# State-space layer: products and scans of four states at a time, through a buffer in SBUF

## The chip, the cores and the metric

The kernel runs on one core of a Trainium2 chip. The metric is the device time of one execution in microseconds (us), the median of several runs. TensorE is PE in the profile, VectorE is DVE, ScalarE is ACT, GpSimd is POOL.

## What is computed

The whole program is an image model of four layers. Only the attention half of layer 2 is touched, a bidirectional state-space (Mamba) layer on 8 images of 257 tokens with 512 inner channels and 32 states:

```python
dt = jax.nn.softplus(jnp.einsum('blr,dr->bld', x_dbl[..., :DT_RANK], Wdt) + bdt)
A = -jnp.exp(Alog)
def step(h, ins):
    dt_t, B_t, C_t, u_t = ins
    dA = jnp.exp(dt_t[..., None] * A)
    h = dA * h + (dt_t * u_t)[..., None] * B_t[:, None, :]
    y = jnp.einsum('bdn,bn->bd', h, C_t)
    return (h, y)
```

It runs once forward and once on the reversed tokens, so there are 16 units of one image and one direction.

## The kernel before, in words

`section_mamba` handles the 16 units one after the other. Channels lie on the 128 partitions in four groups (`j`), states in four groups of eight (`q`). A chunk `n` = 4q + j is eight states of one channel group, 16 chunks to a unit (`NCH`). A chunk is cut into four pairs of states (`m`), and p = 4n + m counts the 64 of them (`SUB`). Each state is a row of L = 256 tokens, so two states are 512 elements on each partition and one PSUM bank.

For two states p, in the steady loop:

- ACT (`decay`, L2326) writes dA = exp(dt * A) into `da`, double-buffered by chunk. The first element of each row stays zero, so that one scan can run over several states in a row.
- PE (`spread_b`, L2114) spreads B over the partitions into the PSUM bank `pb[:, p % 4]` with two matmuls, one for each state. It works two p ahead of the sums that it does for chunk n - 2. It waits on `b_free` for the bank.
- DVE (`product`, L2494) multiplies that bank in place by dt * u (`dtu2`, in SBUF). It does p + 1 ahead of scan p.
- DVE (`body`, L2513) runs the recurrence as a scan of 512 elements: first input `da` in SBUF, second input `pb` in PSUM, output `hs` in SBUF. Before the first scan of chunk n it waits on `hc_done` for POOL to be through with chunk n - 2. The scan raises `b_free`, on which PE, ACT and POOL wait.
- POOL (L2013) multiplies four states of `hs` (1024 elements) by C (`cb`, in SBUF) into `hc`. Both inputs lie in SBUF. There are two to a chunk, and a copy of the last token (L2012) beside them. Between them POOL does other work for the next unit (`taps` L1935, `cut` L1941, `cut_low` and `soften` L1949 to L1960) and for the last token (L1974 to L1995), all of it with SBUF inputs.
- PE (`total`, L2127) adds the states of `hc` into `py` by identity matmuls, two chunks later; its end raises `y_free`, on which POOL waits for the `hc` buffer.

Turned pairs of states are the exception: for m = 3 in state groups q = 1, 2 and 3 (12 of 64 p), DVE makes no product. ACT (`products`, L2348) forms B * dt * u in the other orientation, and PE (`turn_products`, L2101) turns it into `pb` with four transposes of 128x128; the scan reads it from PSUM like the others. `made(p)` counts the products that DVE has made, for the waits on `b_set`.

The order on each engine is written out by hand. Every queue is in order. SP alone issues the DMAs of the layer (`load_c`, `store_c`).

Of the kernel before, what the change touches and what calls it, by code (L numbers as in the profile page):

```python
# [104 lines left out]
def section_constants(nc, k, cls_tok):  # L105
    with nc.Block() as block:
        @block.sync
        def _(sp):
            sp.dma_start(k.cls[:], cls_tok).then_inc(k.loads, 16)
            sp.wait_ge(k.loads, 16)  # L110

        @block.vector
        def _(dve):
            nc.vector.memset(k.ones[:], 1.0)
            nc.vector.memset(k.mean[:], 1.0 / D)
            nc.vector.memset(k.eps[:, 0:1], 1e-5)
# [1665 lines left out]
def section_mamba(nc, k, con, dirs, bfuse, normed=0):  # L1782
# [8 lines left out]
    with ExitStack() as ctx:  # L1791
# [32 lines left out]
        names = ("w_first w_in w_ready eye_set rates in_back out_back proj_done proj_free lead uc_done xd_done xd_out part_set part_cut stacked last_bc last_out rate_l decay_l sum_l y_last z_last dt_done "  # L1824
                 "dt_free dt_exp dt_set crow_in c_out c_even c_odd dtut_done dtut_in tp_in b_done b_free da_done b_set hc_done y_free ys_done o_done o_out "
                 "sqd var std scaled normed f_done f_out conv_link soft_link soft_low soft_top last_link act_head act_tail").split()
# [13 lines left out]
        def made(p):  # L1840
            return sum(not turned(i) for i in range(p + 1))

# [32 lines left out]
        with nc.Block() as block:  # L1875
# [43 lines left out]
            def _(pool):  # L1919
# [77 lines left out]
                def body(u, v, d, before, after):  # L1997
                    scanned, summed = Turn(u, SUB, 4), Turn(u, NCH, 2)
                    for n in range(NCH):
# [49 lines left out]
            def _(pe):  # L2049
# [43 lines left out]
                def turn_products(u, v, p):  # L2093

                    q, j = p // 4 // DJ, p // 4 % DJ
                    if j == 0:
                        pe.wait_ge(s["tp_in"], Turn(u, len(TURNED))(TURNED.index(q) + 1))
                    pe.wait_ge(s["b_free"], Turn(u, SUB, 4)(p - 3))
                    for o in range(2):
                        for h in range(2):  # L2100
                            ins = nc.tensor.transpose(pb[:, p % 4, o, h * P:h * P + P], tp[:, TURNED.index(q) % 2, o, h, j * P:j * P + P], k.ident[:])  # L2101
                    ins.then_inc(s["b_done"], 1)

                def spread_b(u, v, p):

                    if turned(p):
# [4 lines left out]
                    pe.wait_ge(s["b_free"], Turn(u, SUB, 4)(p - 3))  # L2111
# [3 lines left out]
                    ins.then_inc(s["b_done"], 1)  # L2115

# [122 lines left out]
            def _(act):  # L2239
# [78 lines left out]
                def decay(u, v, d, n, m, free):  # L2318
# [3 lines left out]
                    if free is not None:  # L2322
                        act.wait_ge(s["b_free"], free)
                    for o in range(2):
# [13 lines left out]

                def products(u, v, q, o, free):

                    if o == 0:
# [7 lines left out]
                    if o:  # L2349
                        ins.then_inc(s["tp_in"], 1)  # L2350

# [4 lines left out]
                def body(u, v, d, before, after):  # L2356
                    for n in range(NCH):
# [12 lines left out]
                        for m in range(4):  # L2370
                            free = Turn(u, SUB, 4)(4 * (n - 1) + m + 1) if n or before is not None else None
# [6 lines left out]
                        if n == 1:  # L2378
                            for o in range(2):
                                products(u, v, 1, o, Turn(u, SUB)(0) if before is not None else None)  # L2380
                        if n in (5, 7):
                            products(u, v, 2, n // 2 - 2, Turn(u, SUB)(0) if before is not None else None)
                        if n in (9, 10):
                            products(u, v, 3, n - 9, Turn(u, SUB)(32))
                        if after is not None:
# [53 lines left out]
            def _(dve):  # L2439
# [17 lines left out]

                dve.sem_inc(s["b_free"], 4)
                dve.sem_inc(s["y_free"], 2)
# [26 lines left out]

                def product(u, v, p):

                    j = p // 4 % DJ
                    if p < 4 * DJ and p % 4 == 0:  # L2490
                        dve.wait_ge(s["dt_set"], Turn(u, DJ)(j + 1))
                    b2 = pb[:, p % 4]
                    dve.wait_ge(s["b_done"], Turn(u, SUB)(p + 1))
                    nc.vector.tensor_tensor(b2, b2, dtu2[:, v, j:j + 1, 0:L].broadcast_to([P, 2, L]), ALU.mult).then_inc(s["b_set"], 1)  # L2494

                def body(u, v, d, before, after):
                    for n in range(NCH):
                        for m in range(4):
                            p = 4 * n + m
                            if p + 1 < SUB:  # L2500
                                if not turned(p + 1):
                                    product(u, v, p + 1)
                            elif after is not None:
                                product(u + 1, 1 - v, 0)
                            if m == 0:
                                dve.wait_ge(s["hc_done"], Turn(u, 2 * NCH, 16)(2 * n - 2))
                            dve.wait_ge(s["da_done"], Turn(u, SUB)(p + 1))
                            if turned(p):
                                dve.wait_ge(s["b_done"], Turn(u, SUB)(p + 1))
                            else:  # L2510
                                dve.wait_ge(s["b_set"], Turn(u, made(SUB - 1))(made(p)))
                            two = lambda ap: ap.rearrange("p s t -> p (s t)")
                            nc.vector.tensor_tensor_scan(two(hs[:, n % 2, 2 * m:2 * m + 2, :]), two(da[:, n % 2, 2 * m:2 * m + 2, :]), two(pb[:, p % 4]), 0.0, ALU.mult, ALU.add).then_inc(s["b_free"], 1)  # L2513
                            if before is not None:
# [857 lines left out]
def build(nc, a, out, last):  # L3372
    with ExitStack() as ctx:
# [5 lines left out]
        k.x = sb("x", [P, C, B, T])  # L3379
        k.xb = sb("xb", [P, C, TP])  # L3380
        k.cls = sb("cls", [P, C])
# [3 lines left out]
        k.eps = sb("eps", [P, 2])  # L3385
        k.junk = sb("junk", [P, P])
        k.ln_cen, k.ln_sq, k.ln_rstd = sb("ln_cen", [P, C, T]), sb("ln_sq", [P, C, T]), sb("ln_rstd", [P, T])
# [171 lines left out]
```

## Time and profile before

| | us |
|---|---|
| median of 3 runs | 3766.42 (3755.68 to 3770.4) |
| the profiled execution, its own time | 3768.24 |
| its span, first to last instruction | 3766.3 |
| the state-space stage in it, first to last scan and sum | about 1804 (1164.5 to 2968.8) |

The page gives each engine's busy time and share of the span, then the span in 40 slices, in tenths. A group of instructions is written as line, engine, operation, output <- inputs, shape, count, busy time, mean ns of one, idle time of the engine before them and what ended it. [...] Shares over the whole span mix stages with different limits, so the stage has its own windows.

### The profile page before, as it was taken

The page shows a single profiled execution, that of the slowest core. Times are in us where ns is not written, and L with a number is a line of the kernel's source. Part 1 is how long each engine was busy: PE and PEld are TensorE (multiplying, and loading weights), DVE is VectorE, ACT ScalarE, POOL GpSimd, SP SyncE. Part 2 cuts the span into 40 slices and gives each one's busy share as a digit, 9 for nine tenths or more (in the row PEclk, how much of TensorE's full clock was granted, in tenths as well). Part 3 has the DMA queues.
Part 4 walks back from the last instruction along what each step waited for, and adds up shares of the span by engine and source line. Part 5 has one row for each costly group of instructions (what it writes and reads, how often), then busy time and mean ns, then how long its engine had stood idle before and what let it go on. Part 6 is the DMA issues. An engine that isn't in the chain of part 4 may idle for free. (4 is left out here: it accounts for less than half of the span.)

```text
span 3766.3 us, 60909 instructions
## 1 busy us (share of the span) xinstructions
PE 3211.5 (85%) x19844; PEld 2404.9 (64%) x19844; DVE 2513.4 (67%) x3795; ACT 2065.8 (55%) x4488; POOL 1935.6 (51%) x1702
## 2 busy tenths in 40 slices
PE   0959989989986888988888888888988789999767
PEld 0649976668974666666666666666765565666534
DVE  6341136643126999999999999999999644666531
ACT  0332225551227777877777777877776434666511
POOL 0023312101317888889888889898888400000054
PEclk9879989999987999999999999999999998999955
DMA  3039820014951111111111111111111000000045
GB/s 103 2 143 334 323 92 2 2 42 147 333 180 34 46 35 36 46 35 36 46 48 35 49 35 35 47 35 35 46 35 34 23 15 1 2 2 2 18 129 153
DMA packets 133788, 262.81 MB, mean 70 GB/s; under 512 B 14000, under 2 KB 104360, under 8 KB 122952
## 3 DMA queue, kind: packets, MB, share of 16 engines
q1 hardware_dynamic: 122120, 227.64, 18.3%
q0 software_dynamic: 11328, 30.95, 2.5%
q8 instruction: 175, 2.87, 0.3%
q14 instruction: 165, 1.35, 0.1%
HBM read 232.03 MB, written 26.51 MB: 69 GB/s over the span
## 5 line engine op out<-in xcount | busy, mean ns | idle before, releaser
L2013 POOL TENSOR_TENSOR ssm_hc<-ssm_hs,ssm_cb 128x1024 f32<-128x1024 f32 x512 | 1205.2, 2358 | 177.8 <-PE ssm_py L2127 157.8
L2513 DVE TENSOR_TENSOR_SCAN ssm_hs<-ssm_da,ssm_pb 128x512 f32<-128x512 f32 x1024 | 1220.2, 1206 | 97.1 <-POOL ssm_hc L2013 92.4
L2127 PE MATMUL ssm_py<-ssm_hc,ident 128*128 128x256 f32 x4096 | 1071.1, 384 | 40.3 <-POOL ssm_hc L2013 40.3
L2326 ACT ACTIVATE ssm_da<-ssm_dt,ssm_an 128x255 f32<-128x255 f32 x2048 | 863.2, 498 | 191.5 <-DVE ssm_hs L2513 152.4
L2127 PEld LDWEIGHTS ssm_py<-ssm_hc,ident 128*128 128x128 f32 x4096 | 711.4, 192 | 121.1 <-POOL ssm_hc L2013 48.3
L2494 DVE TENSOR_TENSOR ssm_pb<-ssm_pb,ssm_dtu 128x512 f32<-128x512 f32 x832 | 562.7, 676 | 48.3 <-PE ssm_pb L2114 23.8
L2114 PE MATMUL ssm_pb<-ssm_bst,ssm_eyeb 96*128 96x256 bf16 x1664 | 329.1, 280 | 137.3 <-DVE ssm_hs L2513 115.7
L2114 PEld LDWEIGHTS ssm_pb<-ssm_bst,ssm_eyeb 96*128 96x128 bf16 x1664 | 133.8, 99 | 342.7 <-DVE ssm_hs L2513 239.3
L3339 DVE TENSOR_TENSOR moe_hid<-moe_pu,moe_actg 128x512 f32<-128x512 f32 x71 | 49.1, 691 | 349.0 <-PE moe_pu L2982 349.0
L2982 PEld LDWEIGHTS moe_pu<-moe_xt,moe_up 128*128 128x128 f32 x2272 | 267.0, 193 | 6.4 <-ACT moe_xt L3102 3.0
L2982 PE MATMUL moe_pu<-moe_xt,moe_up 128*128 128x128 f32 x2272 | 268.0, 277 | 1.8 <-ACT moe_xt L3102 1.8
L2853 POOL DMA_INDIRECT moe_xr<-moe_x_dram,moe_rowx x71 | 69.0, 971 | 334.6 <-PE ln_ps L2970 179.9
L1662 DVE TENSOR_REDUCE duo_mxr<-duo_pairs 128x4 f32<-128x1024 f32 x128 | 156.6, 1224 | 101.6 <-PE duo_pairs L1400 78.8
L1570 ACT ACTIVATE duo_ex<-duo_pairs 128x1024 f32<-128x1024 f32 x128 | 131.0, 1024 | 99.3 <-PE duo_pairs L1400 99.2
L1396 PE MATMUL duo_pairs<-duo_k,duo_q 32*128 32x256 f32 x1024 | 152.0, 414 | 9.1 <-DVE duo_mxr L1662 3.7
L2101 PE MATMUL ssm_pb<-ident,ssm_tp 128*128 128x128 f32 x768 | 118.8, 278 | 47.8 <-ACT ssm_tp L2348 34.4
L1400 PE MATMUL duo_pairs<-duo_q,duo_k 32*128 32x256 f32 x1024 | 146.3, 402 | 1.2 <-ACT duo_ex L1570 1.1
L2101 PEld LDWEIGHTS ssm_pb<-ident,ssm_tp 128*128 128x128 f32 x768 | 91.7, 141 | 79.4 <-DVE ssm_hs L2513 51.1
L2058 PE MATMUL ln_ps<-x,ssm_win 128*128 (+1 forms) x512 | 135.1, 388 | 3.5 <-DVE x L351 1.8
L2994 PE MATMUL ln_ps<-moe_down,moe_hid 128*128 128x256 f32 x568 | 134.5, 380 | 1.1 <-ACT moe_yo L3120 1.1
L2859 POOL DMA_INDIRECT moe_y_dram<-moe_yo,moe_rowy x71 | 70.2, 988 | 118.9 <-ACT moe_yo L3120 118.9
L2348 ACT ACTIVATE ssm_tp<-ssm_dtut,ssm_bt 128x512 f32<-128x512 f32 x192 | 125.2, 708 | 0.0
(591 smaller groups left out, 5279.1 us busy)
## 6 DMA issues: line engine op xcount, KB each, us to landing
moe_up<-in_moe_up SPq DMA_DIRECT2D x72, 1024.0 KB, 5.4
ssm_cb<-ssm_c_dram SPq DMA_DIRECT2D x64, 1024.0 KB, 5.6
moe_down<-in_moe_down SPq DMA_DIRECT2D x72, 512.0 KB, 6.2
sw_wt<-in_sw_w SPq DMA_DIRECT2D x47, 192.5 KB
moe_x_dram<-moe_tok SPq DMA_DIRECT2D x32, 128.0 KB
moe_yg<-moe_y_dram SPq DMA_DIRECT2D x16, 256.0 KB, 3.4
tok_w<-in_wd SPq DMA_DIRECT2D x4, 576.0 KB, 13.0
out<-h SPq DMA_DIRECT2D x1, 2056.0 KB, 6.3
```

What stands on the lines that cost most here:

```text
L1396: ins1 = nc.tensor.matmul(dst1[:, o, at], q[r, b1, t * P:t * P + P], kk[r, b1, a, 0:256], start=True, stop=True)
L1400: ins2 = nc.tensor.matmul(dst2[:, o, at], kk[r, b2, a, t * P:t * P + P], q[r, b2, 0:256], start=True, stop=True)
L1662: released(nc.vector.tensor_reduce(mxr[:, u % 2, a, 2 * jp:2 * jp + 2, :], bank("s1", u, a, jp).rearrange("p o (t s) -> p o t s", t=2), AX ...
L2013: nc.gpsimd.tensor_tensor(hc[:, n % 2, part_], hs[:, n % 2, part_], cb[:, q % 2, part_, :], ALU.mult).then_inc(s["hc_done"], 1)
L2058: ins = nc.tensor.matmul(pm[:, n % 2, 0:T], w_in[:, c, n * P:n * P + P], row, start=(c == 0), stop=(c == C - 1))
L2101: ins = nc.tensor.transpose(pb[:, p % 4, o, h * P:h * P + P], tp[:, TURNED.index(q) % 2, o, h, j * P:j * P + P], k.ident[:])
L2114: ins = nc.tensor.matmul(pb[:, p % 4, o, :], one_state(st), bst2[:, v, 0:L], start=True, stop=True)
L2127: ins = nc.tensor.matmul(sums(j), k.ident[:], hc[:, n % 2, st, :], start=False, stop=(q == QN - 1 and st == NQ_ - 1 and j % 2 == 1))
L2326: ins = nc.scalar.activation(da[:, n % 2, 2 * m + o, 1:L], dt2[:, v, j, 1:L], ACT.Exp, scale=a_n[:, d, j, st:st + 1])
L2494: nc.vector.tensor_tensor(b2, b2, dtu2[:, v, j:j + 1, 0:L].broadcast_to([P, 2, L]), ALU.mult).then_inc(s["b_set"], 1)
L2513: nc.vector.tensor_tensor_scan(two(hs[:, n % 2, 2 * m:2 * m + 2, :]), two(da[:, n % 2, 2 * m:2 * m + 2, :]), two(pb[:, p % 4]), 0.0, ALU.m ...
L2982: ins = nc.tensor.matmul(pu[:, b % 2, g, j * P:j * P + P], up[:, b % WR, c, g * HID + j * P:g * HID + j * P + P], xt[:, b % 2, c, :], star ...
```

## The change

Scans and products are made for four states (1024 elements, two PSUM banks) instead of two. r counts these half chunks, 32 to a unit (`PAIRS`). The product reads two banks of `pb` and writes a new SBUF buffer `bs` of two halves; the scan takes its second input from `bs`. Turned half chunks are those with r odd in state groups q = 1 and 3, 8 of 32: for them the scan reads the two banks of `pb` straight, and ACT and PE turn four states instead of two. DVE waits ahead of product r + 1 until scan r - 1 is complete, because it writes the buffer which that scan reads. PE waits for its banks on `b_set` (the product has read them) where a product is made, and on `scanned` where it is turned. `scanned` replaces `b_free` for ACT and POOL. The buffers `xb` and `junk`, which nothing reads, and the memset of `xb` at the start go.

```diff
-            nc.vector.memset(k.xb[:], 0.0)
...
+        bs = sb("bs", [P, 2, 4, L])
...
-        TM = 3
-        TURNED = (1, 2, 3)
+        PAIRS = SUB // 2
+        TURNED = (1, 3)
...
-        def turned(p):
-            return p % 4 == TM and p // 4 // DJ in TURNED
+        def turned(r):
+            return r % 2 == 1 and r // 2 // DJ in TURNED
...
-                            pool.wait_ge(s["b_free"], scanned(4 * n + 2 * half + 2))
+                            pool.wait_ge(s["scanned"], scanned(2 * n + half + 1))
...
+                def bank_free(u, r):
+                    if r < 2:
+                        if not (isinstance(u, int) and u == 0):
+                            pe.wait_ge(*((s["scanned"], Turn(u, PAIRS)(0)) if r else (s["b_set"], Turn(u, made(PAIRS - 1))(0))))
+                    elif turned(r - 2):
+                        pe.wait_ge(s["scanned"], Turn(u, PAIRS)(r - 1))
+                    else:
+                        pe.wait_ge(s["b_set"], Turn(u, made(PAIRS - 1))(made(r - 2)))
...
-                    st = q * NQ_ + 2 * TM + o
-                    for h in range(2):
-                        ins = nc.scalar.activation(tp[:, TURNED.index(q) % 2, o, h, :], dtut[:, h, :], ACT.Copy, scale=bt[:, v, h, st:st + 1])
+                    for o in range(2):
+                        st = q * NQ_ + 4 + 2 * i + o
+                        for h in range(2):
+                            ins = nc.scalar.activation(tp[:, i, o, h, :], dtut[:, h, :], ACT.Copy, scale=bt[:, v, h, st:st + 1])
...
-                    nc.vector.tensor_tensor(b2, b2, dtu2[:, v, j:j + 1, 0:L].broadcast_to([P, 2, L]), ALU.mult).then_inc(s["b_set"], 1)
+                    dve.wait_ge(s["b_done"], Turn(u, PAIRS)(r + 1))
+                    if r >= 2 or not (isinstance(u, int) and u == 0):
+                        dve.wait_ge(s["scanned"], Turn(u, PAIRS)(r - 1))
+                    spread = pb[:, at:at + 2].rearrange("p g s t -> p (g s) t")
+                    nc.vector.tensor_tensor(bs[:, r % 2], spread, dtu2[:, v, j:j + 1, 0:L].broadcast_to([P, 4, L]), ALU.mult).then_inc(s["b_set"], 1)
...
+                def scan(u, r):
+                    n, half = r // 2, r % 2
+                    if half == 0:
+                        dve.wait_ge(s["hc_done"], Turn(u, 2 * NCH, 16)(2 * n - 2))
+                    dve.wait_ge(s["da_done"], Turn(u, SUB)(2 * r + 2))
+                    if turned(r):
+                        dve.wait_ge(s["b_done"], Turn(u, PAIRS)(r + 1))
+                        steps = pb[:, 2:4].rearrange("p g s t -> p (g s t)")
+                    else:
+                        dve.wait_ge(s["b_set"], Turn(u, made(PAIRS - 1))(made(r)))
+                        steps = bs[:, half].rearrange("p s t -> p (s t)")
+                    four = lambda ap: ap[:, n % 2, 4 * half:4 * half + 4, :].rearrange("p s t -> p (s t)")
+                    nc.vector.tensor_tensor_scan(four(hs), four(da), steps, 0.0, ALU.mult, ALU.add).then_inc(s["scanned"], 1)
...
+                    for r in range(PAIRS):
+                        n = r // 2
+                        if r + 1 < PAIRS:
+                            if not turned(r + 1):
+                                product(u, v, r + 1)
+                        elif after is not None:
+                            product(u + 1, 1 - v, 0)
+                        scan(u, r)
```

## Rows read from the trace of the kernel before

**Rows 1.** The page: busy time of the engines, then DVE and POOL in 40 slices.

```profile
PE 3211.5 (85%) x19844; PEld 2404.9 (64%) x19844; DVE 2513.4 (67%) x3795; ACT 2065.8 (55%) x4488; POOL 1935.6 (51%) x1702
...
DVE  6341136643126999999999999999999644666531
...
POOL 0023312101317888889888889898888400000054
```

**Rows 2.** Busy time by engine: the stage, one unit, and a stretch far from it.

```profile
1164.50:2968.80 1804.30, 1563.27 (x7956) 1177.53 (x7957) 1686.26 (x1975) 1343.59 (x3036) 1588.80 (x1177) 0.98 0.13 38
1277.30:1390.30 113.00, 97.50 (x505) 73.67 (x504) 105.64 (x125) 85.46 (x193) 100.53 (x76) 1.00 0.13 38
3580.00:3670.00 90.00, 59.32 (x198) 34.80 (x196) 27.77 (x56) 14.86 (x42) 46.70 (x48) 0.52 0.43 125
```

**Rows 3.** Groups of instructions over the span, costliest first.

```profile
L2013 POOL TENSOR_TENSOR ssm_hc<-ssm_hs,ssm_cb 128x1024 f32<-128x1024 f32 x512 | 1205.2, 2358 | 177.8 <-PE ssm_py L2127 157.8
L2513 DVE TENSOR_TENSOR_SCAN ssm_hs<-ssm_da,ssm_pb 128x512 f32<-128x512 f32 x1024 | 1220.2, 1206 | 97.1 <-POOL ssm_hc L2013 92.4
L2494 DVE TENSOR_TENSOR ssm_pb<-ssm_pb,ssm_dtu 128x512 f32<-128x512 f32 x832 | 562.7, 676 | 48.3 <-PE ssm_pb L2114 23.8
L2348 ACT ACTIVATE ssm_tp<-ssm_dtut,ssm_bt 128x512 f32<-128x512 f32 x192 | 125.2, 708 | 0.0
```

**Rows 4.** DVE in order of time, inside a unit: start, us, instruction.

```profile
1510.57 0.68 DVE L2494 TENSOR_TENSOR ssm_pb<-ssm_pb,ssm_dtu 128x512 f32<-128x512 f32 x1
1511.16 1.21 DVE L2513 TENSOR_TENSOR_SCAN ssm_hs<-ssm_da,ssm_pb 128x512 f32<-128x512 f32 x1
1512.28 0.68 DVE L2494 TENSOR_TENSOR ssm_pb<-ssm_pb,ssm_dtu 128x512 f32<-128x512 f32 x1
1512.87 1.21 DVE L2513 TENSOR_TENSOR_SCAN ssm_hs<-ssm_da,ssm_pb 128x512 f32<-128x512 f32 x1
```

**Rows 5.** One line each: duration ns min/median/max, first and last start, shape.

```profile
L276 DVE TENSOR_TENSOR tok_pix<-tok_lo,tok_hi x2: 1217/1221/1225, 65.3 to 67.6; 128x1024 f32<-128x1024 f32 x2
...
L3166 DVE SCALAR_TENSOR_TENSOR x<-x,moe_sc,moe_rstd x16: 472/946/1600, 185.8 to 221.6; 128x257 f32<-128x257 f32 x16
...
L2494 DVE TENSOR_TENSOR ssm_pb<-ssm_pb,ssm_dtu x832: 669/674/700, 1158.8 to 2964.7; 128x512 f32<-128x512 f32 x167
...
L2513 DVE TENSOR_TENSOR_SCAN ssm_hs<-ssm_da,ssm_pb x1024: 1190/1207/1222, 1164.5 to 2967.5; 128x512 f32<-128x512 f32 x171
...
L2013 POOL TENSOR_TENSOR ssm_hc<-ssm_hs,ssm_cb x512: 2337/2357/2379, 1170.0 to 2969.2; 128x1024 f32<-128x1024 f32 x171
```

**Rows 6.** An earlier stage in order of time, DVE beside POOL.

```profile
190.28 0.69 DVE L3163 TENSOR_TENSOR moe_xn<-x,moe_rstd 128x514 f32<-128x514 f32 x1 [2.09 <-ACT moe_rstd L3052]
...
191.01 1.42 DVE L3166 SCALAR_TENSOR_TENSOR x<-x,moe_sc,moe_rstd 128x257 f32<-128x257 f32 x1
...
191.06 1.09 POOL L2846 TENSOR_TENSOR h<-h,moe_xn 128x514 f32<-128x514 f32 x1 [3.74 <-DVE moe_xn L3163]
...
192.35 0.47 DVE L3166 SCALAR_TENSOR_TENSOR x<-x,moe_sc,moe_rstd 128x257 f32<-128x257 f32 x1
```

**Rows 7.** Just before the stage: POOL beside a DVE tensor_scalar, both ways.

```profile
1131.76 1.49 DVE L2455 TENSOR_SCALAR ssm_skip<-ident,ssm_cols 128x128 f32<-128x128 f32 x2
...
1133.05 1.33 POOL L1935 TENSOR_TENSOR ssm_e<-ssm_e,ssm_dt 128x514 f32<-128x514 f32 x1
...
1135.87 1.27 POOL L1935 TENSOR_TENSOR ssm_e<-ssm_e 128x514 f32<-128x514 f32 x1
```

**Rows 8.** Matmul groups of PE in one unit (1277.3 to 1390.3).

```profile
L2127 PE MATMUL ssm_py<-ssm_hc,ident 128*128 128x256 f32 x256 | 66.0, 379 | 2.9 <-POOL ssm_hc L2013 2.9
L2114 PE MATMUL ssm_pb<-ssm_bst,ssm_eyeb 96*128 96x256 bf16 x104 | 20.2, 276 | 8.6 <-DVE ssm_hs L2513 8.3
...
L2101 PE MATMUL ssm_pb<-ident,ssm_tp 128*128 128x128 f32 x48 | 7.4, 276 | 3.0 <-ACT ssm_tp L2348 2.3 <-DVE ssm_hs L2513 0.7
```

More of the change, by code:

```diff
@@ L1824, in section_mamba @@
         names = ("w_first w_in w_ready eye_set rates in_back out_back proj_done proj_free lead uc_done xd_done xd_out part_set part_cut stacked last_bc last_out rate_l decay_l sum_l y_last z_last dt_done "
-                 "dt_free dt_exp dt_set crow_in c_out c_even c_odd dtut_done dtut_in tp_in b_done b_free da_done b_set hc_done y_free ys_done o_done o_out "
+                 "dt_free dt_exp dt_set crow_in c_out c_even c_odd dtut_done dtut_in tp_in b_done scanned da_done b_set hc_done y_free ys_done o_done o_out "
                  "sqd var std scaled normed f_done f_out conv_link soft_link soft_low soft_top last_link act_head act_tail").split()
@@ L1830, in section_mamba, with made @@
         SUB = 4 * NCH
-        TM = 3
-        TURNED = (1, 2, 3)
+        PAIRS = SUB // 2
+        TURNED = (1, 3)
         def sums(j):
             return py[:, j // 2, j % 2 * L:j % 2 * L + L]
-        def turned(p):
-            return p % 4 == TM and p // 4 // DJ in TURNED
-        def made(p):
-            return sum(not turned(i) for i in range(p + 1))
+        def turned(r):
+            return r % 2 == 1 and r // 2 // DJ in TURNED
+        def made(r):
+            return sum(not turned(i) for i in range(r + 1))
         def image(u, d):
@@ L1997, in body @@
                 def body(u, v, d, before, after):
-                    scanned, summed = Turn(u, SUB, 4), Turn(u, NCH, 2)
+                    scanned, summed = Turn(u, PAIRS), Turn(u, NCH, 2)
                     for n in range(NCH):
@@ L2093, in turn_products @@
                 def turn_products(u, v, p):
-                    q, j = p // 4 // DJ, p // 4 % DJ
+                    q, j, i = p // 4 // DJ, p // 4 % DJ, p % 2
                     if j == 0:
-                        pe.wait_ge(s["tp_in"], Turn(u, len(TURNED))(TURNED.index(q) + 1))
-                    pe.wait_ge(s["b_free"], Turn(u, SUB, 4)(p - 3))
+                        pe.wait_ge(s["tp_in"], Turn(u, 2 * len(TURNED))(2 * TURNED.index(q) + i + 1))
                     for o in range(2):
                         for h in range(2):
-                            ins = nc.tensor.transpose(pb[:, p % 4, o, h * P:h * P + P], tp[:, TURNED.index(q) % 2, o, h, j * P:j * P + P], k.ident[:])
-                    ins.then_inc(s["b_done"], 1)
+                            ins = nc.tensor.transpose(pb[:, p % 4, o, h * P:h * P + P], tp[:, i, o, h, j * P:j * P + P], k.ident[:])
+                    if i:
+                        ins.then_inc(s["b_done"], 1)
+                def bank_free(u, r):
[6 more added lines that the diff above has]
+                        pe.wait_ge(s["b_set"], Turn(u, made(PAIRS - 1))(made(r - 2)))
                 def spread_b(u, v, p):
-                    if turned(p):
+                    r = p // 2
+                    if p % 2 == 0:
+                        bank_free(u, r)
+                    if turned(r):
                         turn_products(u, v, p)
@@ L2110, in spread_b @@
                         pe.wait_ge(s["stacked"], u + 1)
-                    pe.wait_ge(s["b_free"], Turn(u, SUB, 4)(p - 3))
                     for o in range(2):
@@ L2114, in spread_b @@
                         ins = nc.tensor.matmul(pb[:, p % 4, o, :], one_state(st), bst2[:, v, 0:L], start=True, stop=True)
-                    ins.then_inc(s["b_done"], 1)
+                    if p % 2:
+                        ins.then_inc(s["b_done"], 1)
                 def total(u, v, d, n, m):
@@ L2322, in decay @@
                     if free is not None:
-                        act.wait_ge(s["b_free"], free)
+                        act.wait_ge(s["scanned"], free)
                     for o in range(2):
@@ L2337, in take_steps, with products @@
                         nc.scalar.copy(dtut[:, h, :], pm[:, h, :]).then_inc(s["dtut_in"], 1)
-                def products(u, v, q, o, free):
-                    if o == 0:
+                def products(u, v, q, i, free):
+                    if i == 0:
                         act.wait_ge(s["last_out"], u + 1)
@@ L2345, in products @@
                             act.wait_ge(s["b_done"], free)
-                    st = q * NQ_ + 2 * TM + o
-                    for h in range(2):
-                        ins = nc.scalar.activation(tp[:, TURNED.index(q) % 2, o, h, :], dtut[:, h, :], ACT.Copy, scale=bt[:, v, h, st:st + 1])
-                    if o:
-                        ins.then_inc(s["tp_in"], 1)
+                    for o in range(2):
+                        st = q * NQ_ + 4 + 2 * i + o
+                        for h in range(2):
+                            ins = nc.scalar.activation(tp[:, i, o, h, :], dtut[:, h, :], ACT.Copy, scale=bt[:, v, h, st:st + 1])
+                    ins.then_inc(s["tp_in"], 1)
                 def decay_last(u):
@@ L2370, in body @@
                         for m in range(4):
-                            free = Turn(u, SUB, 4)(4 * (n - 1) + m + 1) if n or before is not None else None
+                            free = Turn(u, PAIRS)(2 * (n - 1) + m // 2 + 1) if n or before is not None else None
                             if n + 1 < NCH:
@@ L2377, in body @@
                             take_steps(u)
[L2378 to L2384, printed above, removed]
+                        if n in (1, 2):
+                            products(u, v, 1, n - 1, Turn(u, PAIRS)(0) if before is not None else None)
+                        if n in (8, 10):
+                            products(u, v, 3, n // 2 - 4, Turn(u, PAIRS)(PAIRS // 2))
                         if after is not None:
@@ L2456, in _ @@
                 ins.then_inc(s["w_ready"], 1)
-                dve.sem_inc(s["b_free"], 4)
                 dve.sem_inc(s["y_free"], 2)
@@ L2485, in add, with product @@
                     ins.then_inc(s["f_out"], 1)
-                def product(u, v, p):
-                    j = p // 4 % DJ
-                    if p < 4 * DJ and p % 4 == 0:
+                def product(u, v, r):
+                    j, at = r // 2 % DJ, 2 * (r % 2)
+                    if r < 2 * DJ and r % 2 == 0:
                         dve.wait_ge(s["dt_set"], Turn(u, DJ)(j + 1))
-                    b2 = pb[:, p % 4]
-                    dve.wait_ge(s["b_done"], Turn(u, SUB)(p + 1))
-                    nc.vector.tensor_tensor(b2, b2, dtu2[:, v, j:j + 1, 0:L].broadcast_to([P, 2, L]), ALU.mult).then_inc(s["b_set"], 1)
@@ L2496, in body @@
-                def body(u, v, d, before, after):
[L2497 to L2513, printed above, removed]
+                    dve.wait_ge(s["b_done"], Turn(u, PAIRS)(r + 1))
@@ new lines, in product @@
+                    if r >= 2 or not (isinstance(u, int) and u == 0):
[7 more added lines that the diff above has]
+                    dve.wait_ge(s["da_done"], Turn(u, SUB)(2 * r + 2))
+                    if turned(r):
+                        dve.wait_ge(s["b_done"], Turn(u, PAIRS)(r + 1))
[5 more added lines that the diff above has]
+                    nc.vector.tensor_tensor_scan(four(hs), four(da), steps, 0.0, ALU.mult, ALU.add).then_inc(s["scanned"], 1)
@@ L2514, in body @@
+                def body(u, v, d, before, after):
+                    for r in range(PAIRS):
[6 more added lines that the diff above has]
+                        scan(u, r)
+                        for m in (2 * (r % 2), 2 * (r % 2) + 1):
                             if before is not None:
@@ L3379, in build @@
         k.x = sb("x", [P, C, B, T])
-        k.xb = sb("xb", [P, C, TP])
         k.cls = sb("cls", [P, C])
@@ L3385, in build @@
         k.eps = sb("eps", [P, 2])
-        k.junk = sb("junk", [P, P])
         k.ln_cen, k.ln_sq, k.ln_rstd = sb("ln_cen", [P, C, T]), sb("ln_sq", [P, C, T]), sb("ln_rstd", [P, T])
```

## The prediction

> **What bounds the kernel now.** I read the page first: DVE is busy 67% of the span, but nine tenths and more in every slice of the state-space stage, where POOL shows eight tenths [rows 1]. The change touches that stage alone, so the whole-span shares decide nothing. The windows say it in numbers: in 1804.3 us of stage DVE is busy 1686, POOL 1589, PE 1563 and ACT 1344; in one unit of 113 us they are 105.6, 100.5, 97.5 and 85.5 [rows 2]. DVE is the bound; POOL, with 88%, is close behind, and what DVE still idles before its scans is 92 us in which it waits for POOL's product with C [rows 3]. The reader should keep two facts: DVE and POOL are the two fullest engines, and they work beside each other almost all the time. Anything that keeps them from working at the same time costs the sum of both instead of the larger one.
>
> **The change, part by part.** *Fewer, longer DVE instructions.* A product of 512 elements takes 676 ns, a tensor_tensor of 1024 elements takes 1221 [rows 3, 5], so 512 more elements cost about 0.54 us and 0.14 us is fixed. A scan of 512 takes 1206 ns [rows 3]; no longer one is in the trace. With the same fixed 0.14 its elements cost 1.065 us, and 1024 of them give 2.27; twice the row, 2.41, is the upper end, and I take 2.27. But neighbours overlap: from product start to next product start it is 1.71 us [rows 4], 0.59 and 1.12, so in the chain a fixed cost of only some 0.05 us is left of each. Per unit DVE has now 52 products and 64 scans, 52 x 0.59 + 64 x 1.12 = 102.4 us. Then it has 24 products and 32 scans, 24 x 1.12 + 32 x 2.19 = 97.0. That is 5.4 us less per unit.
>
> *DVE's new wait on itself.* Product r + 1 waits for scan r - 1, the instruction directly in front of it, and behind it on DVE stands scan r, which POOL waits for. The nearest row is a dependent pair: L3163 starts at 190.28 and takes 0.69, L3166 waits for it and starts at 191.01, 0.04 behind its end [rows 6], where undisturbed neighbours start 0.1 ahead of it [rows 4]. So it costs about 0.12 us x 24 = 2.9 us per unit; the bounds are 0 and 0.2 x 24 = 4.8. The Trainium skill, "VectorE: DVE Perf Modes", section "The DRAIN you can't avoid", says that a semaphore between DVE instructions costs nothing extra; by that the DVE chain would be 2.9 us per unit shorter than I count. The rows here speak for a small cost.
>
> *The scan's second input moves from PSUM to SBUF.* This carries the sum. Before, each DVE instruction in the loop has one input in SBUF and one in PSUM, and it runs beside POOL with no effect on either: 832 products lie between 669 and 700 ns, 1024 scans between 1190 and 1222, 512 POOL products between 2337 and 2379 [rows 5]. In an earlier stage a DVE instruction with both tensors in SBUF meets a POOL tensor_tensor, and there it is different. The same L3166 on 257 elements takes 0.47 us alone and 1.42 beside POOL; it starts at 191.01, POOL at 191.06 and ends at 192.15, and DVE ends at 192.43, 0.28 later, which is the time that 257 elements stream [rows 6]. So DVE stood still until POOL's instruction was through. The trace holds 16 instructions of L3166, 9 of them beside POOL, and 8 of those 9 took 1.4 to 1.6 us, of all 16 the shortest took 472 ns and the longest 1600 [rows 5]. It goes the other way too: two DVE tensor_scalar end at 1133.25, POOL's L1935 started at 1133.05 and took 1.33 instead of 1.27 us [rows 7]. 0.20 us of overlap cost it 0.06, so 0.14 us of its start is hidden and after that it waits. Both engines thus exclude each other for their streaming time.
>
> After the change 24 of a unit's 32 scans have `da` and `bs`, both in SBUF, and all of POOL's arithmetic reads SBUF. If the scan behaves like L3166, these 384 scans and POOL's work share one resource. A scan holds it for what streams, 2.27 - 0.14 + 0.02 = 2.15 us. POOL is busy 1588.8 us in the stage [rows 2], of which only 5 us are memsets. The sum is 1588.8 + 384 x 2.15 = 2414 us. What makes it less: while a scan holds, the 0.14 us start of the next POOL instruction hides, at most 384 x 0.14 = 54. What makes it more: where POOL has nothing queued it sees the scan's semaphore about 0.1 us late, at most 384 x 0.1 = 38, and the scan may count with its full 2.27, 46 more. So the stage takes 2361 to 2499. Mostly POOL will have something queued, since the 8 scans from PSUM in a unit go beside it and let DVE run ahead until the two `hs` buffers are full; I take 30 hidden and 20 of idle, 2405 us, 150 per unit. The stage grows by 2405 - 1804 = 601 us.
>
> The rule speaks for the step from L3166 to a scan, which no row shows: the Trainium skill, "SBUF — State Buffer", section "Who interferes with whom", says that a DVE instruction with two SBUF inputs contends with a GpSimd instruction that reads SBUF, since its second input comes through the read interface that both share, and whoever is second blocks fully. The trace agrees as far as it goes [rows 6]. By the rule the sum is as above; without it, the next part's 3731.
>
> *What hides under that.* DVE's own work per unit, 24 x 1.21 + 32 x 2.27 = 102 us plus 3 for the small ones, lies under 150. PE makes 96 instead of 104 spreads and 64 instead of 48 transposes; by their rows 20.2/104 and 7.4/48 us [rows 8] that is -1.6 + 2.5, so 0.9 us more on 97.5. ACT makes 16 instead of 12 turned copies of 0.71 us [rows 3], 2.8 more on 85.5. Both have over 45 us of room per unit. If the cover were gone (no exclusion), DVE at about 103 plus waits would still lie above both. The new waits of PE stand ahead of `spread_b`, with the sums of chunk n - 2 queued behind; a product is read out one scan earlier than before, so they come early except for turned half chunks. There PE has from the end of scan r - 2 one scan and one product, 3.4 us, for 8 transposes and 4 sums, 8 x 0.155 + 4 x 0.26 = 2.3 us, which fits. No DMA changes. The memset of `xb` lies at the very start, where DVE then waits for the image; I cost it at nothing (0 to 0.7 us).
>
> **Sum.** 3768.2 for the profiled execution, which is 1.8 above the median of the runs shown, + 601 = 4369. I predict 4370.
>
> **The rivals.** *No exclusion for a scan (12%).* For it: the scan takes two cycles or so per element, 1065 ns for 512, so it is another program than L3166, and no row shows a scan with two SBUF inputs. Against it: L3166 and tensor_scalar, two different operations, are both held. Then DVE saves 5.4 - 2.9 = 2.5 us per unit, 40 in all, with the idle before its scans as it is: 3768 - 40 = 3728 by the sum, 3731 with what a late turned half chunk may cost, 0.2 us per unit. The range of this case is 3680 (no wait on itself, 5.4 x 16 less) to 3790 (scans at 2.41 us: 32 x 0.14 x 16 = 72 more). This is the rival on the other side: it turns on one thing, whether the 24 scans per unit reach SBUF past POOL.
>
> *Partial exclusion (5%).* A scan that takes an element only every second cycle could leave POOL every other turn. Half of the 601 us would then stand: 4070. Against it: L3166 waited for the full POOL instruction, not for parts of it.
>
> *Exclusion, and TensorE's clock falls (5%).* PE would be busy 98 of 150 us. In a stretch where PE is busy 59 of 90 us the granted clock is 0.52, near the 1.2 GHz level; in the stage it is 0.98, near 2.4 GHz [rows 2]. With a mean of 0.6, PE would need 98 / 0.6 = 163 us per unit and be the bound: 3768 + 16 x (163 - 113) = 4568. Against it: a slower PE is busy more of the time, and its gaps here would be a few us at most. It decides from a granted clock of about 98 / 150 = 0.65 down.
>
> **How the numbers follow.** Exclusion with PE in time has 78%, with its own range of 4290 to 4480: the bounds of the sum are 3768 + 557 = 4325 and 3768 + 695 = 4463, and I add 20 to 35 for uneven turns. The range that should hold 8 in 10 is 4150 to 4570; it takes in the third rival, and leaves out the first, the second and some of the likeliest. Half a percent is about what a measurement of this kernel can tell from no change, here 19 us. Slower by more has 78 + 5 + 5 = 88% and 1 from the first rival's top, 89; faster by more (below 3748) has 8, no change 3, from the first rival.
>
> **What would show it.** If right: the 8 scans per unit from `pb` keep about 2.27 us, while those from `bs` show 3 to 4.6 us, often ending one scan's streaming time behind a POOL instruction; POOL's product with C shows a mean well above 2358 ns, 3 to 4.5 us; windows over the stage show DVE and POOL both over 90% busy though a unit takes about 150 us; PE and ACT fall to 65% and 59%. If the first rival holds, scans from `bs` and `pb` are equally long and POOL's stays at 2358. If the third holds, PE's granted clock in the stage is below 0.65 and DVE waits for `b_done`. The forecast is wrong in size if a scan of 1024 elements isn't near 2.27 us or if POOL idles much while DVE makes products.

## The result and the profile after

| | before | after |
|---|---|---|
| median | 3768.41 us (4 runs, 3755.68 to 3771.11) | 4464.9 us (4 runs, 4460.09 to 4486.24) |
| span of the profiled execution | 3766.3 us | 4458.9 us |
| state-space stage, first to last scan | 1804 us | 2498 us |

The ratio is 1.186 with a 95% interval of 1.182 to 1.189. The kernel became slower by 696 us; 601 were forecast. The stage grew by 694 us, which is the whole difference. A unit takes 157.0 us instead of 113.

Windows over the stage and over one unit of the changed kernel (length; busy us and count of PE, PEld, DVE, ACT, POOL; granted TensorE clock; DMA share; GB/s) answer to [rows 2]:

```profile
1159.40:3657.90 2498.50, 1779.12 (x8072) 1353.52 (x8073) 1979.30 (x1014) 1390.97 (x3098) 2150.75 (x1175) 0.87 0.09 28
1316.20:1473.10 156.90, 112.63 (x514) 85.65 (x514) 124.34 (x65) 88.54 (x197) 137.13 (x76) 0.88 0.09 28
```

POOL has the same instructions as before but is "busy" for 2151 us in the stage instead of 1589. It did not get more work: its instructions last longer. The same is seen in the groups (line numbers are shifted), which answer to [rows 3]:

```profile
L2013 POOL TENSOR_TENSOR ssm_hc<-ssm_hs,ssm_cb 128x1024 f32<-128x1024 f32 x512 | 1282.4, 2511 | 158.8 <-DVE ssm_hs L2520 80.2
L2520 DVE TENSOR_TENSOR_SCAN ssm_hs<-ssm_da,ssm_bs 128x1024 f32<-128x1024 f32 x384 | 1220.8, 3183 | 9.0 <-POOL ssm_hc L2013 5.0
...
L2505 DVE TENSOR_TENSOR ssm_bs<-ssm_pb,ssm_dtu 128x1024 f32<-128x1024 f32 x384 | 469.8, 1224 | 531.6 <-PE ssm_pb L2126 483.4
...
L2012 POOL COPY ssm_hl<-ssm_hs 128x8 f32<-128x8 f32 x256 | 240.4, 939 | 164.1 <-DVE ssm_hs L2520 163.1
L2520 DVE TENSOR_TENSOR_SCAN ssm_hs<-ssm_da,ssm_pb 128x1024 f32<-128x1024 f32 x128 | 291.4, 2277 | 0.0
```

The two groups of scans stand side by side in one kernel, same length, same output: from `pb` in PSUM 2277 ns, from `bs` in SBUF 3183. A single line's spread (min/median/max ns) makes it plainer still, also for two small operations of POOL:

```profile
L2520 DVE TENSOR_TENSOR_SCAN ssm_hs<-ssm_da,ssm_bs x384: 2259/3208/4429, 1159.4 to 3653.4; 128x1024 f32<-128x1024 f32 x192
L2520 DVE TENSOR_TENSOR_SCAN ssm_hs<-ssm_da,ssm_pb x128: 2276/2277/2287, 1203.7 to 3655.6; 128x1024 f32<-128x1024 f32 x128
...
L2012 POOL COPY ssm_hl<-ssm_hs x256: 181/193/2200, 1171.8 to 3660.5; 128x8 f32<-128x8 f32 x128
...
L1941 POOL TENSOR_TENSOR ssm_rank<-ssm_rank,ssm_part x32: 628/2623/2657, 1138.9 to 3458.3; 32x257 f32<-32x257 f32 x32
```

And the timeline shows the two engines taking turns (start, us, instruction), POOL first, then DVE:

```profile
1632.69 2.35 POOL L2013 TENSOR_TENSOR ssm_hc<-ssm_hs,ssm_cb 128x1024 f32<-128x1024 f32 x1
...
1635.01 4.35 POOL L2013 TENSOR_TENSOR ssm_hc<-ssm_hs,ssm_cb 128x1024 f32<-128x1024 f32 x1
...
1639.30 2.19 POOL L2012 COPY ssm_hl<-ssm_hs 128x8 f32<-128x8 f32 x1
...
1634.11 3.09 DVE L2520 TENSOR_TENSOR_SCAN ssm_hs<-ssm_da,ssm_bs 128x1024 f32<-128x1024 f32 x1
...
1637.43 1.21 DVE L2505 TENSOR_TENSOR ssm_bs<-ssm_pb,ssm_dtu 128x1024 f32<-128x1024 f32 x1
1638.56 2.94 DVE L2520 TENSOR_TENSOR_SCAN ssm_hs<-ssm_da,ssm_bs 128x1024 f32<-128x1024 f32 x1
1641.61 1.23 DVE L2505 TENSOR_TENSOR ssm_bs<-ssm_pb,ssm_dtu 128x1024 f32<-128x1024 f32 x1
```

POOL's first product ends at 1635.04. The scan that had started at 1634.11 ends at 1637.20, 2.16 us after that. POOL's second product, "running" since 1635.01, ends at 1639.36, again 2.16 us after the scan. The next scan ends at 1641.50, 2.14 later, and the copy of 8 elements beside it, which alone takes 0.19 us, ends at 1641.49. Only DVE's product, which reads PSUM and one SBUF tensor, goes through beside POOL in 1.21 us. The rest of the stage looks the same: of the 384 scans from `bs`, 342 took over 2.4 us with the end of a POOL instruction inside them, and each of these ends 2.14 or 2.16 us behind that end. None waited for two POOL instructions.

### The profile page after: what moved, and what is told of

The parts are those of the page before. It is cut to its first block and busy times, and to the rows that moved or that the text cites. A ratio compares the mean times of both kernels' runs of the same rounds, so it can differ in the third digit from the quotient of the medians.

```text
span 4458.9 us, 58923 instructions
## 1 busy us (share of the span) xinstructions
PE 3427.2 (77%) x19972; PEld 2582.0 (58%) x19972; DVE 2808.2 (63%) x2834; ACT 2112.9 (47%) x4552; POOL 2499.5 (56%) x1702
## 5 line engine op out<-in xcount | busy, mean ns | idle before, releaser
L2013 POOL TENSOR_TENSOR ssm_hc<-ssm_hs,ssm_cb 128x1024 f32<-128x1024 f32 x512 | 1282.4, 2511 | 158.8 <-DVE ssm_hs L2520 80.2
L2520 DVE TENSOR_TENSOR_SCAN ssm_hs<-ssm_da,ssm_bs 128x1024 f32<-128x1024 f32 x384 | 1220.8, 3183 | 9.0 <-POOL ssm_hc L2013 5.0
L2140 PE MATMUL ssm_py<-ssm_hc,ident 128*128 128x256 f32 x4096 | 1189.0, 418 | 11.0 <-POOL ssm_hc L2013 11.0
L2140 PEld LDWEIGHTS ssm_py<-ssm_hc,ident 128*128 128x128 f32 x4096 | 787.8, 212 | 114.1 <-POOL ssm_hc L2013 16.6
L2505 DVE TENSOR_TENSOR ssm_bs<-ssm_pb,ssm_dtu 128x1024 f32<-128x1024 f32 x384 | 469.8, 1224 | 531.6 <-PE ssm_pb L2126 483.4
L2100 PE MATMUL ssm_pb<-ident,ssm_tp 128*128 128x128 f32 x1024 | 190.1, 317 | 344.8 <-DVE ssm_hs L2520 316.1
L2100 PEld LDWEIGHTS ssm_pb<-ident,ssm_tp 128*128 128x128 f32 x1024 | 140.5, 163 | 408.3 <-DVE ssm_hs L2520 354.6
L2012 POOL COPY ssm_hl<-ssm_hs 128x8 f32<-128x8 f32 x256 | 240.4, 939 | 164.1 <-DVE ssm_hs L2520 163.1
L2520 DVE TENSOR_TENSOR_SCAN ssm_hs<-ssm_da,ssm_pb 128x1024 f32<-128x1024 f32 x128 | 291.4, 2277 | 0.0
L2362 ACT ACTIVATE ssm_tp<-ssm_dtut,ssm_bt 128x512 f32<-128x512 f32 x256 | 162.8, 707 | 0.0
```

Source lines behind the costliest of these rows:

```text
L2012: nc.gpsimd.tensor_copy(h_l[:, v, j, q * NQ_:(q + 1) * NQ_], hs[:, n % 2, :, L - 1])
L2013: nc.gpsimd.tensor_tensor(hc[:, n % 2, part_], hs[:, n % 2, part_], cb[:, q % 2, part_, :], ALU.mult).then_inc(s["hc_done"], 1)
L2140: ins = nc.tensor.matmul(sums(j), k.ident[:], hc[:, n % 2, st, :], start=False, stop=(q == QN - 1 and st == NQ_ - 1 and j % 2 == 1))
L2362: ins = nc.scalar.activation(tp[:, i, o, h, :], dtut[:, h, :], ACT.Copy, scale=bt[:, v, h, st:st + 1])
L2505: nc.vector.tensor_tensor(bs[:, r % 2], spread, dtu2[:, v, j:j + 1, 0:L].broadcast_to([P, 4, L]), ALU.mult).then_inc(s["b_set"], 1)
L2520: nc.vector.tensor_tensor_scan(four(hs), four(da), steps, 0.0, ALU.mult, ALU.add).then_inc(s["scanned"], 1)
```

## The experiments

Each kernel is compared with the kernel before on the same chip (3749 to 3786 us there). The kernels did not all run on one chip, so differences between two of them are read from the stages of their profiles (first to last scan), unless both ran on the same chip. The stages, in the order of the runs below: 2568, 2271, 1738, 2657, 2435, 1904, 1863 and 1861 us, against 1804 before and 2498 after the change.

**One part of the change alone.** To the kernel before, only the buffer is added, with DVE's wait on itself that it needs (the unused `xb` and `junk` go too):

```diff
+        bs = sb("bs", [P, 2, 2, L])
...
-                    nc.vector.tensor_tensor(b2, b2, dtu2[:, v, j:j + 1, 0:L].broadcast_to([P, 2, L]), ALU.mult).then_inc(s["b_set"], 1)
+                    dve.wait_ge(s["b_free"], Turn(u, SUB, 4)(p - 1))
+                    nc.vector.tensor_tensor(bs[:, p % 2], b2, dtu2[:, v, j:j + 1, 0:L].broadcast_to([P, 2, L]), ALU.mult).then_inc(s["b_set"], 1)
...
-two(pb[:, p % 4])
+two(pb[:, p % 4] if turned(p) else bs[:, p % 2])
```

> The kernel before, with one part of the change alone: the product goes to a buffer in SBUF and the scan reads it from there, still two states at a time, with the turned pairs as they were. Exclusion of DVE and POOL: 52 scans per unit stream 1.09 us each while POOL stands, and POOL gets only one half-length scan between two of its instructions, so a unit takes 160 to 170 us and the time is 4500 to 4700 us; scans from the buffer show 2 us and more, those from PSUM 1.21. Rival, the loss comes from the wide instructions and their order: then only DVE's wait on itself is added, 52 x 0.12 us per unit, and the time stays under 3880 us.

Measured 4538 us, ratio 1.201 (1.189 to 1.213). The scans (min/median/max ns):

```profile
L2514 DVE TENSOR_TENSOR_SCAN ssm_hs<-ssm_da,ssm_bs x832: 1191/2253/3404, 1167.7 to 3733.0; 128x512 f32<-128x512 f32 x167
L2514 DVE TENSOR_TENSOR_SCAN ssm_hs<-ssm_da,ssm_pb x192: 1189/1210/1214, 1221.5 to 3734.2; 128x512 f32<-128x512 f32 x192
```

A unit takes 159 to 164 us. The buffer alone costs more than the whole change (a stage of 2568 us against 2498; the intervals of the two ratios just touch); neither the width of four states nor the new order of TensorE is needed for the loss.

**POOL's reads taken away.** In the changed kernel, and in the kernel before as its control, POOL's product with C and its copy become memsets of the same tiles. The sums over states are left out by that.

```diff
-                                nc.gpsimd.tensor_copy(h_l[:, v, j, q * NQ_:(q + 1) * NQ_], hs[:, n % 2, :, L - 1])
-                            nc.gpsimd.tensor_tensor(hc[:, n % 2, part_], hs[:, n % 2, part_], cb[:, q % 2, part_, :], ALU.mult).then_inc(s["hc_done"], 1)
+                                nc.gpsimd.memset(h_l[:, v, j, q * NQ_:(q + 1) * NQ_], 0.0)
+                            nc.gpsimd.memset(hc[:, n % 2, part_], 0.5).then_inc(s["hc_done"], 1)
```

> The changed kernel; POOL's product with C and its copy of the last token are replaced by memsets of the same tiles, which read nothing in SBUF (the sums over states are left out). Exclusion by reads: the 384 scans from the buffer fall to 2.28 us except beside POOL's other work (24 us per unit), and the time falls by over 400 us, to 3900 to 4050: DVE's chain of 103 us per unit, some 6 for what POOL still reads, and 2.3 us before each of 8 products per unit for which TensorE is late. If the scans were slow by themselves, or by the wait of DVE on itself, they would stay at 3.2 us and the time above 4300.

> The kernel before with the same memsets in POOL, as the control of the last one. Both theories: DVE's chain of 105 us per unit with few waits, 3640 to 3700 us. Only the distance from this one to the changed kernel with memsets tells what the change costs apart from POOL's reads: I expect 230 to 400 us.

Measured 4257 us for the changed kernel and 3716 us for the kernel before, both with memsets. The scans of the changed one:

```profile
L2520 DVE TENSOR_TENSOR_SCAN ssm_hs<-ssm_da,ssm_bs x384: 2265/2281/3375, 1181.9 to 3446.9; 128x1024 f32<-128x1024 f32 x192
```

Their median fell from 3208 to 2281 ns. Only 78 of the 384 still take over 2.35 us, and each of them lies beside one of POOL's other instructions, which still read SBUF. The memsets are also shorter than the product (0.95 us instead of 2.36), but that isn't why: 157 scans ran over at least a part of one and stayed under 2.35 us. A memset that begins under a scan isn't held, nor is the scan; DVE's timeline and then POOL's:

```profile
2004.07 2.27 DVE L2520 TENSOR_TENSOR_SCAN ssm_hs<-ssm_da,ssm_bs 128x1024 f32<-128x1024 f32 x1
...
2004.30 0.10 POOL L2012 MEMSET ssm_hl<- 128x8 f32 x1 [1.63 <-DVE ssm_hs L2520]
2004.34 0.95 POOL L2013 MEMSET ssm_hc<- 128x1024 f32 x1
```

So the mechanism held, but the time did not: it fell by 208 us (the stage by 228) and not by over 400, and the distance to the control is 541 us and not 230 to 400. The control lies 16 us above its range. DVE's idle time ahead of products tells where the rest is:

```profile
L2505 DVE TENSOR_TENSOR ssm_bs<-ssm_pb,ssm_dtu 128x1024 f32<-128x1024 f32 x384 | 469.9, 1224 | 645.5 <-PE ssm_pb L2126 603.4
```

603 us of waiting for TensorE, 38 per unit; the expectation had put 2.3 x 8 = 18 on it. The cause is a loop. In the quarters with turned half chunks, TensorE turns r only when scan r - 2 has freed the banks; the spread for r + 1 lies behind that in its queue; product r + 1 waits for the spread; and scan r lies behind product r + 1 on DVE. TensorE's part of the loop in the changed kernel, from the release of the bank at 1609.21 (the scan's end) to the last spread, after which the product starts at 1614.12:

```profile
1609.21 0.66 PE L2100 MATMUL ssm_pb<-ident,ssm_tp 128*128 128x128 f32 x4 [2.65 <-DVE ssm_hs L2520]
1609.70 1.03 PE L2140 MATMUL ssm_py<-ssm_hc,ident 128*128 128x256 f32 x4
...
1611.26 0.66 PE L2100 MATMUL ssm_pb<-ident,ssm_tp 128*128 128x128 f32 x4
...
1613.70 0.38 PE L2126 MATMUL ssm_pb<-ssm_bst,ssm_eyeb 96*128 96x256 bf16 x2
```

That is 4.9 us, with 12 sums and a few small matmuls between. Together with 1.14 us of product and 2.2 of scan the loop takes about 8.3 us for two half chunks, where DVE has 5.5 us of work.

**More locked scans, no turned ones.** The changed kernel with `TURNED = ()`, without ScalarE's and TensorE's work for it.

> The changed kernel with no half chunk turned: all 32 scans per unit read the buffer in SBUF, TensorE and ScalarE do less. Exclusion: POOL's 99.3 us and 32 x 2.15 us share one resource, 168 us per unit, less some 4 hidden and with 2 to 5 idle: 4600 to 4700 us. Rival, TensorE's late turned halves (483 us of DVE's idle time) set the time: without them it falls below 4300 us.

Measured 4626 us, its stage 2657 us, 166 to 170 us per unit. By the sum of the prediction, with 512 scans: 1589 + 512 x 2.15 = 2690 us, 33 more than measured. The loop just described is gone, and yet the stage is 159 us longer: 8 x 2.15 us more of locked scan in each unit would make 275, and that the difference is what the loop had cost is argued, not measured. DVE still waits 335 us for spreads here, while the time lies below the sum, so DVE's idle time alone doesn't tell what a wait costs. The rival fell.

**TensorE's order.** The changed kernel; TensorE spreads for r + 1 before it turns r:

```diff
                 def spread_b(u, v, p):
                     r = p // 2
+                    if turned(r) and r < PAIRS - 1:
+                        p, r = p + 2, r + 1
+                    elif r and turned(r - 1):
+                        p, r = p - 2, r - 1
...
-                    dve.wait_ge(s["b_done"], Turn(u, PAIRS)(r + 1))
+                    dve.wait_ge(s["b_done"], Turn(u, PAIRS)(r if r and turned(r - 1) else r + 1))
...
-                        dve.wait_ge(s["b_done"], Turn(u, PAIRS)(r + 1))
+                        dve.wait_ge(s["b_done"], Turn(u, PAIRS)(r + 2 if r < PAIRS - 1 else r + 1))
```

> The changed kernel; TensorE spreads B for half chunk r + 1 before it turns half chunk r, so that the product r + 1, which DVE makes ahead of scan r, does not wait for transposes that need a bank first. If the 90 us above the forecast (stage 2498 against 2405) are this order, the idle time of DVE before products falls from 532 us to under 200 and the time to 4360 to 4420. If POOL and the locked scans fill the time anyway, or the idle time only moves to the scans, it stays at 4450 to 4475.

Measured 4384 us, ratio 1.170 (1.167 to 1.174) against 1.186. The stage in one window, its form as in [rows 2]:

```profile
1157.80:3592.40 2434.60, 1806.28 (x8071) 1357.13 (x8072) 2051.76 (x1014) 1389.25 (x3098) 2154.85 (x1175) 0.86 0.10 28
```

And DVE's products and scans on its page:

```profile
L2524 DVE TENSOR_TENSOR_SCAN ssm_hs<-ssm_da,ssm_bs 128x1024 f32<-128x1024 f32 x384 | 1287.9, 3357 | 137.5 <-POOL ssm_hc L2013 114.8
...
L2509 DVE TENSOR_TENSOR ssm_bs<-ssm_pb,ssm_dtu 128x1024 f32<-128x1024 f32 x384 | 469.4, 1223 | 206.6 <-PE ssm_pb L2130 158.1
...
L2524 DVE TENSOR_TENSOR_SCAN ssm_hs<-ssm_da,ssm_pb 128x1024 f32<-128x1024 f32 x128 | 291.6, 2278 | 58.7 <-PE ssm_pb L2100 57.0
```

The stage is 64 us shorter, 30 above the 2405 forecast. The idle time before products fell by 325 us, from 532 to 207, but only a fifth of that reached the end. Some 187 us came back as idle time before scans, 110 of it in waits for POOL's product with C, and 67 us as longer locked scans (384 of them, a mean of 3357 ns instead of 3183).

**Both together.** TensorE's order and POOL's memsets (the sums over states are left out).

> The same order of TensorE, and POOL's product with C and its copy replaced by memsets (the sums over states are left out). Nothing but POOL's other work excludes the scans then: DVE's chain of 103 us per unit and some 6 for that, 3700 to 3760 us; so against the kernel before with the same memsets the wide instructions bring nothing, within 60 us. Rival: the order matters little and it stays within 50 us of the changed kernel with memsets.

Measured 3851 us, 119 us per unit, against 4257 without the new order and 3716 for the control, both on another chip. In the stage, with most of POOL's reads gone, the order is worth 366 us, with them 64. The rival here fell, but the expectation's upper end was 91 us too low: DVE still idles 170 us before products and 87 before scans from `pb`, of which 206 are waits for TensorE. In the stage four states at a time lose 167 us to two, even so; about 36 of them are scans that POOL's other instructions still lengthen (a mean of 2374 ns instead of 2281).

**Four states at a time without the buffer.** Product in place in PSUM, scan from there; product r is made directly ahead of scan r, so that TensorE can fill banks during a scan.

```diff
-                    nc.vector.tensor_tensor(bs[:, r % 2], spread, dtu2[:, v, j:j + 1, 0:L].broadcast_to([P, 4, L]), ALU.mult).then_inc(s["b_set"], 1)
+                    nc.vector.tensor_tensor(spread, spread, dtu2[:, v, j:j + 1, 0:L].broadcast_to([P, 4, L]), ALU.mult).then_inc(s["b_set"], 1)
...
-                        steps = bs[:, half].rearrange("p s t -> p (s t)")
+                        steps = pb[:, 2 * half:2 * half + 2].rearrange("p g s t -> p (g s t)")
...
-                        if r + 1 < PAIRS:
-                            if not turned(r + 1):
-                                product(u, v, r + 1)
-                        elif after is not None:
-                            product(u + 1, 1 - v, 0)
+                        if not turned(r):
+                            product(u, v, r)
```

TensorE waits on `scanned` for every bank then.

> The changed kernel without the buffer: four states at a time, product in place in PSUM and scan from there, and the product r is made after scan r - 1, so TensorE has the length of one scan to fill its banks. Exclusion: no scan is lengthened, all 512 take 2.28 us and POOL's product with C 2.36; TensorE needs 2.1 to 2.5 us for spreads and sums against 2.2, so DVE idles 0 to 0.5 us per half chunk: 3740 to 3880 us. If four states at a time are slow for another reason than the buffer, POOL's instructions are still lengthened and it stays above 4200 us.

Measured 3808 us, ratio 1.018 (1.013 to 1.022). All scans and POOL's products (min/median/max ns) are undisturbed, beside each other as before:

```profile
L2512 DVE TENSOR_TENSOR_SCAN ssm_hs<-ssm_da,ssm_pb x512: 2259/2286/2290, 1158.2 to 3018.7; 128x1024 f32<-128x1024 f32 x171
...
L2012 POOL TENSOR_TENSOR ssm_hc<-ssm_hs,ssm_cb x512: 2335/2355/2380, 1162.9 to 3022.9; 128x1024 f32<-128x1024 f32 x171
```

Of the 18.6% that the change costs 1.8% is left, with the wide instructions kept. DVE is busy 1641 us in the stage instead of 1686, but it idles more than it saves: before scans 151 us, before products 76, where it was 97 and 25. The rival, that four states at a time are slow for another reason than the buffer, falls.

**TensorE's spreads ahead of its sums.** The same, with `spread_b` called for both pairs of a half chunk before the sums.

> The run without the buffer once more, with TensorE doing all four spreads or eight transposes of a half chunk before the sums, instead of two in between. If TensorE's lateness is what keeps four states at a time from paying, DVE's 73 us of waiting for spreads falls by half or more, and the time to 3730 to 3770 us, about that of the kernel before. If the idle time moves to the scans (POOL's product with C, 96 us), it stays at 3790 to 3810.

Measured 3816 us, ratio 1.018 (1.014 to 1.021). The groups of DVE:

```profile
L2513 DVE TENSOR_TENSOR_SCAN ssm_hs<-ssm_da,ssm_pb 128x1024 f32<-128x1024 f32 x512 | 1160.0, 2281 | 212.1 <-POOL ssm_hc L2012 146.2 <-ACT ssm_da L2334 40.6 <-PE ssm_pb L2099 8.3
L2498 DVE TENSOR_TENSOR ssm_pb<-ssm_pb,ssm_dtu 128x1024 f32<-128x1024 f32 x384 | 465.8, 1213 | 40.4 <-POOL ssm_dtu L1959 22.2 <-PE ssm_pb L2120 15.5 <-issue 2.6
```

The waiting for spreads fell from 73 to 16 us, and waiting for POOL's product with C rose from 96 to 146. The time did not move. No kernel with four states at a time beat the kernel before.

## Why the prediction was right, and where its sizes were off

*The scan's second input.* Right. The sum had taken an exclusion seen on two other operations over to the scan. Only one of the two, L3166, reads two tensors; the `tensor_scalar` of [rows 7] reads one tensor and one value per partition, so it says nothing of a second tensor input. For the scan it is shown by three runs: the buffer alone brings the loss, taking it away with four states kept removes nearly all of it, and taking POOL's reads away brings the scans back to 2281 ns. The Trainium skill, "SBUF — State Buffer", section "Who interferes with whom", says that a DVE instruction with two SBUF inputs contends with a GpSimd instruction that reads SBUF and not with one that only writes; the trace agrees for both halves, 3208 against 2281 ns of median. The price of 2.15 us per locked scan was right to 0.01 in the timeline, in part by luck: 2.27 - 0.14 is 2.13, and no row stood behind the 0.02 that was added.

*The stage's length.* 2405 us forecast, 2498 measured. Apart from 1589 + 384 x 2.15 = 2414 I had taken 30 off for hidden starts and 20 on for idle time, -10 in all; it was +84. The step that failed is in "What hides under that": TensorE was given one scan and one product, 3.4 us, for 8 transposes and 4 sums of 2.3 us. But the next product stands ahead of that scan on DVE, and its spreads stand behind the transposes on TensorE, so the window was one scan and the work 4.9 us. With the order mended the same difference is +20, with no turned half chunks it is -33. So 64 of the 93 us are that step, shown by one run; what the other 29 are stays open. That 2498 still lies at the edge of the sum's own bounds, 2361 to 2499, is luck, since they held no term for this wait. Starts of POOL's instructions that hide under a scan are consistent with the -33, but that is argued.

*Fewer, longer instructions.* The length of a scan of 1024, 2.27 us, was measured as 2.277, and a product's 1.21 as 1.224. 5.4 us less per unit were forecast for the instructions, 2.5 after DVE's wait on itself. In the run without the buffer DVE's busy time in the stage, which counts overlapped stretches once, fell by 46 us, 2.9 per unit. Each scan waits there for the product right in front of it, so this run can't tell the two terms apart.

*DVE's wait on itself.* It was put at 0.12 us and measures 0.18 where nothing else stands between: in the changed kernel a product starts 0.10 us behind the end of the scan that it waits for (175 of 384; in the timeline above 1641.61 behind 1641.50), where undisturbed neighbours overlap by 0.08. That is inside the bounds of 0 to 0.2, and it is not the zero that was weighed against it.

*The first rival's time.* It was never the case, but its price was too good: 3731 us would have needed that TensorE keeps up. With POOL's product and copy as memsets the change as written stands 541 us above its control, with the mended order too its stage is 167 us above, and the run without the buffer is at 1.018. So without the exclusion the change as written would most likely not have been faster. The rival's range to 3790 was too narrow above, since the late turned halves cost 24 us per unit there (143 against 119 us) and not 0.2. Its top was also added up wrongly: 3728 + 72 is 3800.

*Signs.* The scans from `pb` kept 2277 ns, those from `bs` 2.26 to 4.43 us, as told. POOL's product with C was to show 3 to 4.5 us and shows 2511 ns: only 44 of the 512 had to wait for a scan. POOL's other waits fell on its small instructions and other work: a copy of 8 elements, 0.19 us alone, and `cut`, 0.65 us alone, took over 2 us. DVE and POOL were to be over 90% busy, and are 79% and 86%. PE was to fall to 65% and is at 71%: its clock was granted at 0.87 instead of 0.98, and one sum takes 418 ns instead of the 379 of [rows 8]. That is above the third rival's 0.65, and DVE's 483 us of waiting for spreads is not it: the mended order removed two thirds of it with the clock at 0.86. The median of 4465 lies in the range of 4150 to 4570 and in the likeliest case's own, 4290 to 4480; the growth was 95 us more than the forecast's 601.

## What to carry to other kernels

Before you move an operand of a VectorE instruction from PSUM to SBUF, count its SBUF inputs and look at what GpSimd does at that moment: with two on the one side and reads on the other, both engines together took nearly the sum of their times here, however small the single instructions were. When two engines' queues are written out by hand, follow a new wait around the whole loop, through what is queued in front of the instruction on each engine; an instruction that comes ahead of the one you are costing may need something from behind the slow one. And longer instructions save only the part of the fixed cost that isn't overlapped already, here about 0.05 us of 0.14.

## What was not expected of the hardware

An instruction of 8 elements on GpSimd can be held for a whole scan of VectorE: 193 ns of median, 2200 at most. A held instruction is shown as busy, so shares of busy time rise while less is done: POOL shows 2151 us for work of 1589. The two engines took turns: no locked scan of the stage had to let two POOL instructions pass, and no product with C took over 4.36 us, about its own 2.35 and one scan. And the granted clock of TensorE fell little with its load: PE was busy 87% of the stage before and 71% after, and the granted clock went from 0.98 to 0.87 (96% and then 74% of the stage at 2.4 GHz, the rest at 1.2), though in [rows 2] a stretch with 66% has 0.52.
